# The last gate of a gated cross-attention and mixture-of-experts kernel: order of the group ranking changed

## What is computed

```python
# layer 3, x2d: [2048, 256]; wg: [256, 8]; C = 256
x = x + tanh(g_xattn[3]) * attention(q=layernorm(x), k=ctx, v=ctx)
logits = layernorm(x).reshape(-1, 256) @ wg
gates = softmax(logits)
idx = argmax(gates)
mask = one_hot(idx, 8)
loc = cumsum(mask, axis=0) - 1          # place of the token in its expert
mask = mask * (loc < C)
gate_s = sum(gates * mask)              # weight of the token
# dispatch rows by (expert, place), h = relu(rows @ w1[e]), out = h @ w2[e]
x = x + tanh(g_ffn[3]) * (gate_s * out, back in token order)
```

## Time and profile before

| | us |
|---|---|
| median of 3 runs | 984.86 |
| the profiled execution | 981.5 |
| its span | 979.8 |
| layer 3's gate begins | 769.6 |
| last scatter of token rows starts | 848.06 |
| experts' first work on TensorE | 853.47 |

### The profile page before, as it was taken

How to read it: one execution, slowest core, us unless ns; L and a number is a source line. 1 busy time by engine, 2 the same in 40 slices (tenths; PEclk the granted TensorE clock), 3 DMA queues, 4 the chain that set the end, 5 groups by cost and what they waited for, 6 DMA issues and landing times. The chain is left out here.

```text
span 979.8 us, 15133 instructions
## 1 busy us (share of the span) xinstructions
PE 853.3 (87%) x5751; PEld 650.5 (66%) x5758; DVE 445.9 (46%) x1216; ACT 357.3 (36%) x731; POOL 197.8 (20%) x198
## 2 busy tenths in 40 slices
PE   6988999999999968999999999756779797399996
PEld 5764666578888845666766766533556576288885
DVE  3775544300323045777667555326666487300000
ACT  2332212212322225544545455435668333022221
POOL 1217100022433200001001000003445223412122
PEclk9996999999999969999999999968889998599998
DMA  6033700053654380000000000000000011435451
GB/s 217 24 129 128 264 1 22 22 188 115 213 168 147 56 310 1 2 1 1 2 1 2 1 1 2 1 0 1 1 0 1 1 44 65 133 117 172 123 183 20
DMA packets 33872, 70.55 MB, mean 72 GB/s; under 512 B 9219, under 2 KB 23947, under 8 KB 28940
## 3 DMA queue, kind: packets, MB, share of 16 engines
q1 hardware_dynamic: 26937, 59.92, 17.3%
q0 software_dynamic: 6144, 8.31, 4.4%
q10 hardware_dynamic: 722, 1.39, 0.4%
HBM read 54.98 MB, written 14.80 MB: 71 GB/s over the span
## 5 line engine op out<-in xcount | busy, mean ns | idle before, releaser
L589 PE MATMUL banks<-arena 32*120 32x256 f32 (+6 forms) x1808 | 163.2, 379 | 16.1 <-DVE small L1886 13.1
L1205 ACT ACTIVATE arena<-banks 128x512 f32<-128x512 f32 (+4 forms) x159 | 92.6, 598 | 198.2 <-PE banks L1011 34.7
L589 PE MATMUL banks<-ffw,arena 128*128 128x256 f32 (+2 forms) x633 | 125.2, 355 | 16.4 <-DVE x L1997 15.0
L589 PEld LDWEIGHTS banks<-arena 32*120 32x120 f32 (+5 forms) x1808 | 102.1, 164 | 51.1 <-issue 31.5
L589 PEld LDWEIGHTS banks<-ffw,arena 128*128 128x128 f16 (+1 forms) x640 | 87.2, 140 | 47.2 <-issue 23.6
L589 PE MATMUL banks<-arena,ew 128*128 128x256 f32 x512 | 114.9, 383 | 1.4 <-ACT arena L1205 1.4
L589 PE MATMUL banks<-ew,arena 128*128 128x256 f32 x512 | 113.2, 379 | 0.0
L589 PEld LDWEIGHTS banks<-arena,ew 128*128 128x128 f32 x512 | 98.3, 192 | 15.6 <-ACT arena L1205 2.0
L589 PEld LDWEIGHTS banks<-ew,arena 128*128 128x128 f32 x512 | 96.2, 190 | 12.5
L1886 DVE TENSOR_REDUCE small<-banks 128x16 f32<-128x1920 f32 x32 | 69.0, 2158 | 25.8 <-PE banks L589 25.6
L1383 ACT ACTIVATE arena<-banks,mcol 120x2048 f32<-120x2048 f32 x32 | 63.1, 1971 | 19.5 <-PE banks L589 19.5
(11 more groups left out here) (237 smaller groups left out, 1243.4 us busy)
## 6 DMA issues: line engine op xcount, KB each, us to landing
ew<-in_w SPq DMA_DIRECT2D x32, 1024.0 KB, 7.2
xrow<-arena SPq DMA_DIRECT2D x1, 2064.0 KB, 21.8
arena<-xrow SPq DMA_DIRECT2D x8, 258.0 KB, 4.6
zrow<-arena SPq DMA_DIRECT2D x8, 256.0 KB, 2.2
ffw<-in_shared SPq DMA_DIRECT2D x2, 1024.0 KB, 7.3
acc<-x SPq DMA_DIRECT2D x4, 512.0 KB, 2.9
ffw<-in_tern SPq DMA_DIRECT2D x2, 1024.0 KB, 8.8
out<-x SPq DMA_DIRECT2D x8, 256.0 KB, 2.0
```

The costliest lines, as they stand in the source:

```text
L589: return pe.matmul(o, l, r, start=a, stop=b)
L1205: return nc.scalar.activation(o, i_, ACT.Copy)
```

## The change

On TensorE, the loop of layer 3 ends after step 7, and what is left is written out: `turn_p(7)`, `values(7)`, then turn and logits of blocks 6 and 7 back to back, then the ranks of groups 2 and 3. Groups 0 and 1 are ranked at the end of steps 5 and 7, behind the logits of blocks 3 and 5. The ranks of group 0 stay in bank 4, and `turn_p(5)` instead of `turn_p(6)` waits for `take_ranks(0)`; those of the other groups go to bank 0, a bank of the keys, and no longer wait for the copy of the probabilities. On VectorE, group 0 is picked in step 5 and group 1 in step 7, both ahead of `add_output`; the ranks of group 0 are read at the start of step 6 and its slots found behind `shift(6)`; behind step 7 the rest is written out, with `take_ranks(1)` first, then the last addition to x, and `find_slots(1)` behind the statistics of block 7. On GpSimd the six scatters of group 0 go to steps 6 and 7, ahead of the power for the gate of blocks 5 and 6. On ScalarE the exponentials of groups 0 and 1 go to the ends of steps 5 and 7. No instruction is added or removed but some waits. Layer 0 keeps its order.

```diff
--- before.py
+++ after.py
@@ -432,11 +432,11 @@
                 for s in range(NB + 1):
                     if s + 1 < NB:
                         rstd_of(one, s + 1, 0)
-                    if L == 3 and s in (7, 8):
-                        if s == 7:
+                    if L == 3 and s in (6, 7):
+                        if s == 6:
                             g.wait_ge(ex["blank"], 16)
                             g.wait_ge(gt["slot"], 1)
-                        for t in range(3 * (s - 7), 3 * (s - 6)):
+                        for t in range(3 * (s - 6), 3 * (s - 5)):
                             move(t)
                     if 1 <= s:
                         rstd_of(gt, s - 1, 1)
@@ -682,7 +682,7 @@
                     pe.wait_ge(q["p_sb"], b0 + k + 1)
                     if k >= 1:
                         pe.wait_ge(q["pT_sb"], b0 + k)
-                    if L == 3 and k == 6:
+                    if L == 3 and k == 5:
                         pe.wait_ge(gt["rank_sb"], 1)
                     for t in range(TB):
                         m = pe.transpose(psum[4][0:SK, t * P:(t + 1) * P], P1[:, k % 2, t, :], ident[:, :])
@@ -726,8 +726,9 @@
                     pe.wait_ge(gt["picked"], n + 1)
                     if n >= 1:
                         pe.wait_ge(gt["rank_sb"], n)
-                    pe.wait_ge(one["pT_sb"], b0 + (6 if n == 0 else NB))
-                    o = psum[4][:, 256:256 + w * E].rearrange("p (t e) -> p t e", t=w)
+                    if n == 0:
+                        pe.wait_ge(one["pT_sb"], b0 + 5)
+                    o = (psum[0] if n else psum[4])[:, 256:256 + w * E].rearrange("p (t e) -> p t e", t=w)
                     m = mm(o, tri[:, :], sel[:, t0:t1, :], True, False)
                     for t in range(t1 - 1):
                         f = max(t + 1 - t0, 0)
@@ -738,7 +739,7 @@
                 if L == 0:
                     pe.wait_ge(load["values"], 32)
                 keys_values(0)
-                for s in range(NB + 2):
+                for s in range(NB + 2 if L == 0 else NB):
                     if s < NB:
                         turn_z(s)
                     if 1 <= s <= NB:
@@ -751,11 +752,17 @@
                         gate_turn(s - 2)
                     if 1 <= s <= NB:
                         values(s - 1)
-                    if L == 3 and s in (6, 8, 9):
-                        group_ranks((6, 8, 9).index(s))
                     if 2 <= s:
                         logits(s - 2)
+                    if L == 3 and s in (5, 7):
+                        group_ranks(s // 2 - 2)
                 if L == 3:
+                    turn_p(NB - 1)
+                    values(NB - 1)
+                    for k in (NB - 2, NB - 1):
+                        gate_turn(k)
+                        logits(k)
+                    group_ranks(2)
                     group_ranks(3)
 
             one_gate(0)
@@ -1281,8 +1288,8 @@
                         exps(s)
                     if 2 <= s:
                         take_gate_z(s - 2)
-                    if L == 3 and s in (6, 8, 9):
-                        group_exp((6, 8, 9).index(s))
+                    if L == 3 and s in (5, 7, 9):
+                        group_exp(s // 2 - 2)
                 if L == 0:
                     act.wait_ge(rt["logit"], 1)
                     nc.scalar.activation(prob, logit, ACT.Exp).then_inc(rt["prob_exp"], 1)
@@ -1613,7 +1620,9 @@
                     v.wait_ge(load["values"], 32)
                     v.wait_ge(su["tanh"], 1)
                 take_values(0)
-                for s in range(NB + 3):
+                for s in range(NB + 3 if L == 0 else NB):
+                    if L == 3 and s == 6:
+                        take_ranks(0)
                     if s + 1 < NB:
                         if s == 1:
                             v.wait_ge(load["x"], 16 * (1 + L // 3))
@@ -1622,25 +1631,37 @@
                         normalize(gt, s - 2, 1, z2)
                     if s < NB:
                         shift(s)
+                    if L == 3 and s == 6:
+                        find_slots(0)
                     if 3 <= s:
                         take_logits(s - 3)
                     if s + 1 < NB:
                         normalize(one, s + 1, 0, z)
+                    if L == 3 and s in (5, 7):
+                        pick_expert(s // 2 - 2)
                     if 1 <= s <= NB:
                         add_output(s - 1)
                     if s + 1 < NB:
                         take_values(s + 1)
-                    if L == 3 and s in (6, 8):
-                        take_ranks(s // 2 - 3)
                     if 1 <= s <= NB:
                         stats(gt, s - 1, 1)
-                    if L == 3 and s in (6, 8):
-                        find_slots(s // 2 - 3)
-                    if L == 3 and s in (5, 7, 9, 10):
-                        pick_expert((5, 7, 9, 10).index(s))
-                    if L == 3 and s >= 9:
-                        take_ranks(s - 7)
-                        find_slots(s - 7)
+                if L == 3:
+                    take_ranks(1)
+                    add_output(NB - 1)
+                    normalize(gt, NB - 2, 1, z2)
+                    v.drain()
+                    stats(gt, NB - 1, 1)
+                    take_logits(NB - 3)
+                    find_slots(1)
+                    normalize(gt, NB - 1, 1, z2)
+                    take_logits(NB - 2)
+                    pick_expert(2)
+                    take_logits(NB - 1)
+                    take_ranks(2)
+                    find_slots(2)
+                    pick_expert(3)
+                    take_ranks(3)
+                    find_slots(3)
                 if L == 3:
                     return
                 q = rt
```

## The result

The changed kernel takes 993.24 us (median of 5 runs, 990.91 to 995.77) against 985.78 us of the kernel before (median of 5, 984.52 to 987.44): a ratio of 1.0073, interval 1.0049 to 1.0098, or 5 to 10 us more. The direction was as forecast, the size was not: the forecast was 988.1, with a range up to 990.8.

What follows compares the result with a forecast made beforehand. The last scatter's start, hanging on the slots of group 1, was taken as the bound. Delays through steps 6, 7 and the tail moved it from 848.06 to 851.3: 984.9 + 3.2 = 988.1 us, range 984.0 to 990.8 with the rivals.

Steps and rivals of the forecast that it cites:

- What bounds the kernel: End of layer 3: only the last scatter's start (848.06 us) moves the time; it hangs on the slots of group 1.
- Step 6, the wait: TensorE: `turn_p(5)` waits for `take_ranks(0)` and starts 2.9 us later, so `shift(6)` starts 2.44 us later.
- Which clock: When TensorE's clock falls: never before the scatters +0.4 us, from about 828 +3.2, already from 816 up to +6.4.
- the middle one: TensorE's clock is low from about 828 as before: +3.2 us, the course taken, chance 0.57.
- low clock early: Rival, chance 0.15: TensorE's clock falls already in step 6; +4.8 to +6.4 us, 989.7 to 991.3 us.
- upper end: Clock already low from 816: at most doubles step 6's 3.82 us, of which 3.2 are work; +6.4 us in all.
- Step 7: GpSimd's scatters 0 to 2 stand ahead of its power for block 5's gate; `shift(7)` at 826.5, 3.1 us later.
- The tail: After `shift(7)`: `add_output(7)` ahead of `find_slots(1)` loses the earlier ranking; group 2 second bound, last scatter at 851.3, low clock.
- High clock in the tail: Rival, chance 0.15: the clock stays high in the tail; +0.4 us, 985.3 us, no measurable change.
- The hidden wait: Rival, chance 0.13: `turn_p(5)` finds the ranks taken, VectorE's two waits don't arise; -2.8 us, 982.1 us.
- The other rule weighed in the prediction: GpSimd contends with VectorE's two-input instructions: six scatters would cost 0.8 us more in GpSimd's queue; left out of the sum.

Runs made afterwards that it cites:

- with 12 products: Changed kernel with 12 unread 128x128 products on TensorE in front of the wait of `turn_p(5)`; 989.98 us, ratio 1.0061 against the kernel before.
- d_again: Second run of the tail alone: new tail, group 0 picked, ranked and sent as in the kernel before; 983.0 us, ratio 0.9995.
- e3_slots_first: Changed kernel with `find_slots(1)` right behind `take_ranks(1)`, ahead of the last addition to x; 992.14 us, ratio 1.0078 against the kernel before.
- bank 7 kernel: Changed kernel with the ranks of group 0 in bank 7 instead of 4, so `turn_p(5)` needs no wait; 987.29 us, ratio 1.001 against the kernel before.
- d_tail_only: First run of the tail alone: new tail, group 0 picked, ranked and sent as in the kernel before; 987.47 us, ratio 1.0003.
- e2_filler: Changed kernel with 20 unread 128x128 products on TensorE in front of the wait of `turn_p(5)`; 989.93 us, ratio 1.0042 against the kernel before.
- c_head_only: Kernel before with only group 0 picked, ranked and sent one step sooner, `turn_p(5)` waiting for its ranks in bank 4; 995.83 us, ratio 1.0093.

## Why the prediction was right and wrong

**What bounds the kernel: right.** The last scatter's start sets when the experts begin: in all 14 profiles TensorE starts their first product 7.0 to 7.6 us later. That nothing else moves was nearly right: from the last scatter to the end it is 131.5 to 133.2 us. A gain did need earlier slots of group 1 and group 2 within 5.1 us of them: the kernel that met both is the only one faster than before.

**Step 6, the wait: right.** Forecast 2.44 us at `shift(6)`; with the clock kept high it is 49.9 - 47.1 = 2.8. `turn_p(5)` was forecast at 45.7 and came at 46.1.

**Which clock: this is the step that failed.** Three courses were priced, and the prediction took the middle one, a fall only at 828, because that row was nearest in place and length. The idle stretch of 2.67 us before `turn_p(5)` was enough, in five profiles of five, and the fall to 1.2 GHz came inside it. The rival *low clock early* had the mechanism and a chance of 0.15. The reason for the choice doesn't hold in its own row either: the stretch before 829.56 begins at 826.47, and windows of 1 us give TensorE 1.00, 0.90 and 0.50 from 826 on, so there too the fall came in the first half of the stretch.

The price of that fall was right: +3.2 in the upper end, 3.4 us measured at `shift(6)`, and 3.3 at the last scatter (86.5 against 83.2 with the stretch filled). Even so the rival's +4.8 to +6.4 us stayed under the 8.0 and 9.2 measured at the last scatter, because the middle course under it was too small. With the stretch filled it measures 4.7 and not 3.2. From the forecast of 81.7 to 86.5 the terms are: 0.3 for the wait, 3.4 for the clock, 0.4 in step 7, 1.0 from `shift(7)` to the slots of group 1, and 0.3 back in the gap before group 2. The 1.0 does not come from the early fall: the changed kernel takes 12.4 us there and was forecast 11.4, and the kernels with bank 7, with 20 and with 12 products take the same 12.4, though their clock had stayed high through step 6. In all four `gate_turn(5)`, late behind the delayed power, finds the clock low: `values(6)` take 1.91 us and `logits(5)` 1.71, and `turn_p(7)` starts 4.4 us behind `gate_turn(5)`. With the old head (d_again) these 4.4 us are 2.8, at the high clock, and the 12.4 are 9.9.

**Step 7: nearly right.** From `shift(6)` to `shift(7)` the forecast was 7.35 us; it was 7.79 in both profiles of the changed kernel. The mechanism, GpSimd's scatters ahead of its power, is shown by VectorE's wait of 1.41 us; the sum had 0.9 for it (826.5 - 825.6).

**The tail: half right.** The gap before group 2 was forecast at 1.7 us. It was 80.2 - 73.7 - 5.1 = 1.4 in the second profile and 2.5 in the first. That the order on VectorE loses the earlier ranking was wrong, as e3_slots_first showed: with early slots the power of block 7 bounds instead. And the tail is no loss: behind an undisturbed head it brings the slots of group 1 from 66.7 to 65.5 and 63.7 (two profiles). The prediction never priced it by itself. One sum in it is off by 0.2 us (838.8 + 3.67 is 842.5), which changes nothing here.

**The rivals.** *High clock in the tail* did not occur: every profile is at the low clock before the last ranks. *The hidden wait* is what the bank 7 kernel builds, without its gain: slots of group 1 at 68.0 and not 63.6, the last scatter at 82.2 and not 75.3 to 75.9. It had taken the wait for the power of block 5 to go away too, and that wait is 1.41 us there, as in the changed kernel.

The Trainium skill (TensorE: Matmul & The Clock Gate, HAM oscillation — how this bites in real kernels) describes bursts of products between waits, each of which starts at the slow clock. The trace agrees for an ordinary semaphore wait on another engine: 0.74 granted in the window with the wait, 0.50 behind it. It does not for every wait: behind 2.12 us in d_again the clock is still at 1.00 (last section). The other rule weighed in the prediction, that GpSimd and VectorE contend, has next to no trace here. The prediction read 1.09 and 0.96 us as VectorE busy and idle, but the length goes by place: the first scatter of a row takes 1.03 to 1.16 us, the third and later ones 0.95 or 0.96 whether VectorE is busy or not (the changed kernel's third, at 832.55, with VectorE busy beside it). The later steps of a row are 1.26 to 1.31 us, before and after. One scatter, the first behind the power of block 5 (834.46), takes 1.16 where the kernel before has 1.03.

**What stays open.** Between the end of the ranks of group 2 and `take_ranks(2)` lie 1.15 us in the first profile of the changed kernel (852.15 to 853.30, with VectorE idle) and 0.04 in the second. The same 1.1 stands in the profiles of d_tail_only, e1_bank7 and e2_filler (0.35 in c_head_only), and 0.04 in those of all later runs, d_again among them. So it belongs to neither kernel nor order; what it is, these runs don't tell. It makes the difference between 86.5 and 87.7. Open is also why the profile of the bank 7 kernel shows 3.7 us of loss at the last scatter and its ten runs 1.1. And these rows give no length of idle time that the clock bears (last section).

## What to carry over

Price a new wait twice: by its length, and by the clock of what stands behind it on TensorE. Here the wait cost 2.8 us and the low clock behind it 3.4, and with what stood behind the delayed power the head came to 9.7 at the last scatter. Sending work earlier on an in-order queue pays only if what it is put ahead of can wait; here nobody waited for group 0, and the power behind its scatters was waited for. What did pay, together with the new tail, was 0.5 us of ranks (and their reading on VectorE) moved ahead of 1.9 us of logits that were needed later.

## What the runs showed of the hardware

The fall of TensorE's clock beside the idle stretch of 2.67 us was not expected; in the row before it the engine was busy 3.31 of 4 us at 2.4 GHz. Both rows behind it are busy throughout (8.00 us) at 1.2 GHz; the next is granted 0.89, and from 832 on it is 0.51 again. That second fall has an idle stretch of only 0.52 us before it (831.51). On the other hand the tail alone (d_again) keeps the high clock through an idle stretch of 2.12 us, with TensorE busy 3.42 of the 4 us before it:

```profile
832.70 0.66 PE L708 MATMUL banks<-ident,arena 128*128 128x128 f32 x4 [2.12 <-DVE arena L1533]
```

So in these rows the length of an idle stretch alone does not tell whether the clock falls. The stall of VectorE in c_head_only, 4.36 us from the end of the ranks to their reader with nothing in the core to explain it, was not expected either.
